# Graph attention kernel: 1,536 of the gathered rows are loaded one by one by SyncE and ScalarE, and the ring of gather buffers has 12 slots in place of 16

## The reference

```python
Q_h = (x @ Wq + bq).reshape(N, H, D)      # K_h, V_h alike
E = (edge_attr @ We + be).reshape(-1, H, D)
score = K_h[src_idx] * Q_h[dst_idx] / jnp.sqrt(D) * E
score = jnp.exp(jnp.clip(score.sum(-1, keepdims=True), -5.0, 5.0))
wV = segment_sum(V_h[src_idx] * score, dst_idx, N)
Z = segment_sum(score, dst_idx, N)
h_out = (wV / (Z + 1e-06)).reshape(N, H * D)
return layernorm(x + h_out)
```

## Time and profile before

| | |
|---|---|
| median of three runs | 1004.61 us |
| profiled execution | 1004.89 us, of it the span of the core 1003.1 us |
| GpSimd busy | 742.9 us (74%), 790 instructions |
| TensorE busy | 754.7 us (75%) |
| VectorE busy | 595.4 us (59%) |
| ScalarE busy | 453.4 us (45%) |
| DMA engines, mean share busy | 50 to 60% through the loop over groups |

### The profile page before, as it was taken

How to read it: one execution, slowest core, us unless ns; L and a number is a source line. 1 busy time by engine, 2 the same in 40 slices (tenths; PEclk the granted TensorE clock), 3 DMA queues, 4 the chain that set the end, 5 groups by cost and what they waited for, 6 DMA issues and landing times.

```text
span 1003.1 us, 13052 instructions
## 1 busy us (share of the span) xinstructions
PE 754.7 (75%) x3387; PEld 418.3 (42%) x3387; DVE 595.4 (59%) x1584; ACT 453.4 (45%) x1096; POOL 742.9 (74%) x790
## 2 busy tenths in 40 slices
PE   5899987877777777777876686777768778777763
PEld 4656643433443334343433343434435334343332
DVE  4459965555555655565556556565565656565664
ACT  3477754444444444444435345334444444444421
POOL 6777777777777777777777777777777777777772
PEclk9999998789789898979788989888887987889885
DMA  8997775555555555555554655555545555555321
GB/s 222 310 238 194 203 190 156 155 152 155 147 150 144 141 155 132 143 137 161 133 148 134 157 141 133 158 133 147 151 129 151 149 150 141 140 141 158 99 80 45
DMA packets 124294, 153.03 MB, mean 153 GB/s; under 512 B 57725, under 2 KB 91967, under 8 KB 124212
## 3 DMA queue, kind: packets, MB, share of 16 engines
q0 software_dynamic: 36944, 75.08, 29.7%
q1 hardware_dynamic: 80448, 73.74, 25.8%
q10 hardware_dynamic: 6822, 3.31, 1.3%
HBM read 142.06 MB, written 9.98 MB: 152 GB/s over the span
## 4 chain that ended last, share of the span: by engine, by line
POOL 64%; issue 21%; PE 5%; DMA 4%; DVE 3%; SPq 1%; ACT 0%; POOLq 0%; DVEq 0%
POOL kv L472 64%; DMA kv<-kv_table,src_idx 2%; DMA q_table<-node_stage 1%; DMA w_all<-biases_in 1%; PE ps_eq L902 1%; PE ps_eq L957 1%; SPq L393 1%; PE ps_qe_seg L902 1%; PE ps_eq L950 1%; DMA q_win<-q_table 1%; PE ps_last L902 0%; DVE node_stage L712 0%; SPq L397 0%; DVE ps_last L737 0%; PE ps_eq_qe L902 0%
## 5 line engine op out<-in xcount | busy, mean ns | idle before, releaser
L472 POOL DMA_INDIRECT kv<-kv_table,src_idx x746 | 706.2, 947 | 227.6 <-issue 225.4
L571 ACT ACTIVATE ps_last<-clipped 128x32 f32<-128x32 f32 x196 | 39.4, 201 | 489.2 <-DVE clipped L744 484.6
L957 PE MATMUL ps_eq<-pick_t,q_win 128*96 128x512 f32 (+1 forms) x262 | 156.3, 682 | 18.8 <-ACT e_t L566 17.5
L950 PE MATMUL ps_eq<-ea,w_all 128*96 128x512 f32 (+1 forms) x262 | 161.4, 703 | 8.2 <-DVE qe_t L720 6.6
L730 DVE TENSOR_TENSOR kq<-kv,ps_qe_seg 128x384 f32<-128x384 f32 x98 | 53.9, 550 | 180.2 <-DMA kv<-kv_table,src_idx 180.0
L730 DVE TENSOR_TENSOR kq<-kv,ps_eq_qe 128x384 f32<-128x384 f32 x98 | 54.1, 552 | 176.4 <-DMA kv<-kv_table,src_idx 176.4
L981 PE MATMUL ps_qe_seg<-node_stage 128*104 128x80 f32 x784 | 104.1, 284 | 52.4 <-DVE acc_t L766 38.0
L981 PE MATMUL ps_last<-node_stage 128*104 128x80 f32 x780 | 99.9, 277 | 56.9 <-DVE acc_t L766 48.2
L557 ACT ACTIVATE distance<-rel_bc,neg_part 80x512 bf16<-80x512 bf16 x196 | 138.4, 706 | 2.0 <-issue 1.0
L560 ACT ACTIVATE pick_t<-distance 80x512 f32<-80x512 bf16 x196 | 123.2, 629 | 6.2
L981 PEld LDWEIGHTS ps_qe_seg<-node_stage 128*104 128x104 f32 x784 | 94.0, 198 | 60.7 <-DVE node_stage L751 45.0
(11 more groups left out here) (85 smaller groups left out, 663.5 us busy)
## 6 DMA issues: line engine op xcount, KB each, us to landing
ea<-ea_t_in SPq DMA_DIRECT2D x196, 192.0 KB
rel_bc<-rel_rows_dram SPq DMA_DIRECT2D x196, 80.0 KB
kv<-kv_table,src_idx POOLq DMA_INDIRECT x746
q_win<-q_table SPq DMA_DIRECT2D x196, 30.0 KB
kv_table<-node_stage SPq DMA_DIRECT2D x5, 960.0 KB, 6.1
x_both<-x_t_in SPq DMA_DIRECT2D x5, 480.0 KB, 12.4
q_table<-node_stage SPq DMA_DIRECT2D x5, 480.0 KB, 7.6
x_both<-x_rows_in ACTq DMA_DIRECT2D x10, 240.0 KB, 3.5
```

Of the source, the lines that this page charges most:

```text
L472: pool.indirect_dma_start(rows[0:n, :], None, table, bass.IndirectOffsetOnAxis(ap=src_idx[0:n, tile:tile + 1], axis=0)).then_inc(semaphore ...
L950: nc.tensor.matmul(ps_eq[2 * group % 3][0:DIM, 0:n], w_e, ea[:, slot, 0:n], start=True, stop=True).then_inc(e_e, 1)
L957: nc.tensor.matmul(ps_eq[(2 * group + 1) % 3][0:DIM, 0:n], q_win[:, slot, :], pick_t[:, group % 3, 0:n], start=True, stop=True).then_inc(e ...
```

## The change

Groups 98 and 190 are no longer gathered by GpSimd. SyncE loads their 1,024 rows, each with a DMA of its own from `kv_table`, 22 in each quad from the first quad on. ScalarE does the same for the 512 rows of group 178, 12 in each quad, three after the exponentials of each group. The node numbers come as two further inputs and are loaded into registers once for each quad. The three groups have buffers and semaphores of their own, and the ring for the 193 groups left to GpSimd has 12 slots. VectorE waits for the four tiles of such a group on four semaphores.

```diff
-KV_RING, EA_RING, REL_RING, QWIN_RING, PICK_RING, MSG_RING = 16, 8, 8, 8, 4, 4
+KV_RING, EA_RING, REL_RING, QWIN_RING, PICK_RING, MSG_RING = 12, 8, 8, 8, 4, 4
+SYNC_GROUPS, SYNC_ROWS = (98, 190), 22
+SCALAR_GROUPS, SCALAR_ROWS = (178,), 12
+ROW_GROUPS = sorted(SYNC_GROUPS + SCALAR_GROUPS)
+POOL_GROUPS = [group for group in range(GROUPS) if group not in ROW_GROUPS]
...
+def rows_in(quad, groups, per_quad):
+    rows = [(group, row) for group in groups for row in range(GROUP)]
+    return rows[quad * per_quad:(quad + 1) * per_quad]
...
+        def load_row(eng, group, row, number):
+            t, p = divmod(row, P)
+            eng.dma_start(kv[p:p + 1, kv_slot(group), t, :], kv_table[bass.ds(number, 1), :]
+                          ).then_inc(e_rows[group][t], 16)
...
 @@ SyncE's loop @@
                 for quad in range(QUADS):
-                    for group, base in enumerate(bases_of(mybir.EngineType.SP, quad), quad * QUAD):
+                    rows = rows_in(quad, SYNC_GROUPS, SYNC_ROWS)
+                    loaded = numbers_of(quad, QUAD + len(rows))
+                    for i in range(QUAD):
...
-                        load_window(group, base)
+                        load_window(group, loaded[i])
+                        for (row_group, row), number in [*zip(rows, loaded[QUAD:])][i::QUAD]:
+                            load_row(sp, row_group, row, number)
...
 @@ GpSimd's loop @@
-                for group in range(EARLY, GROUPS):
-                    slot = group % KV_RING
-                    if group >= KV_RING:
-                        pool.wait_ge(e_msg, group - KV_RING + 1)
+                for i, group in enumerate(POOL_GROUPS[EARLY:], EARLY):
+                    if i >= KV_RING:
+                        pool.wait_ge(e_msg, POOL_GROUPS[i - KV_RING] + 1)
...
 @@ ScalarE's first DMAs, and its loop @@
             act.dma_start(dst_idx[:], dst_cols).then_inc(l_dst, 16)
+            act.dma_start(numbers[:, :, QUAD:], src_sync).then_inc(l_numbers, 16)
+            act.dma_start(act_numbers[:], src_scalar).then_inc(l_act_numbers, 16)
...
                     if group < GROUPS:
                         exponentials(group)
+                    if group % QUAD == 0 and rows_in(group // QUAD, SCALAR_GROUPS, SCALAR_ROWS):
+                        loaded = numbers_of(group // QUAD)
...
+                    for row_group, row in rows_at(group):
+                        load_row(act, row_group, row, loaded.pop(0))
```

More of the change, by code:

```diff
@@ L96, in edges_in, with kv_slot, kv_fetched @@
     return min(P, N_EDGES - tile * P)
+def kv_slot(group):
+    return KV_RING + ROW_GROUPS.index(group) if group in ROW_GROUPS else POOL_GROUPS.index(group) % KV_RING
+def kv_fetched(group):
+    slot, last = kv_slot(group), POOL_GROUPS.index(group)
+    return sum(tiles_of(POOL_GROUPS[i]) for i in range(slot, last + 1, KV_RING))
+def rows_in(quad, groups, per_quad):
+    rows = [(group, row) for group in groups for row in range(GROUP)]
+    return rows[quad * per_quad:(quad + 1) * per_quad]
 def steps_at(group, lag, streamed):
@@ L137, in build @@
     assert SUMS * FINAL_TILES + WINDOW <= 512 and LAG_TRANSPOSE == SUMMED + 2
+    for groups, rows in ((SYNC_GROUPS, SYNC_ROWS), (SCALAR_GROUPS, SCALAR_ROWS)):
+        for i, group in enumerate(groups):
+            assert EARLY <= QUAD * -(-(i + 1) * GROUP // rows) < group < GROUPS - 1
     assert EARLY < KV_RING and tiles_of(EARLY) == GROUP_TILES
@@ L287, in build @@
         e_kv = [sem(f"e_kv{i}") for i in range(KV_RING)]
+        e_rows = {group: [sem(f"e_rows{group}_{t}") for t in range(GROUP_TILES)] for group in ROW_GROUPS}
         e_ea = [sem(f"e_ea{i}") for i in range(EA_RING)]
@@ L540, in _ @@
             act.wait_ge(c_float, 2)
+            act.wait_ge(l_act_numbers, 16)
             path = path_of(act)
@@ L598, in finish_nodes, with numbers_of, rows_at @@
                         normalise(step)
+            def numbers_of(quad):
+                return list(nc.values_load_multi_w_load_instructions(
+                    act_numbers[0:1, quad, 0:len(rows_in(quad, SCALAR_GROUPS, SCALAR_ROWS))],
+                    engines=[mybir.EngineType.Activation], min_val=0, max_val=N_NODES,
+                    skip_runtime_bounds_check_because=IN_TABLES)[1])
+            def rows_at(group):
+                rows = rows_in(group // QUAD, SCALAR_GROUPS, SCALAR_ROWS)
+                first, last = (len(rows) * (group % QUAD + i) // QUAD for i in range(2))
+                return rows[first:last]
             def windowed(streamed):
+                all_tables_stored(act)
                 make_pick_t(0)
@@ L723, in times_keys @@
             def times_keys(group):
-                n, slot = tiles_of(group), group % KV_RING
-                fetched = sum(tiles_of(g) for g in range(slot, group + 1, KV_RING))
-                dve.wait_ge(e_kv[slot], 16 * fetched)
+                n, slot = tiles_of(group), kv_slot(group)
+                if group in ROW_GROUPS:
+                    for t in range(n):
+                        dve.wait_ge(e_rows[group][t], 16 * P)
+                else:
+                    dve.wait_ge(e_kv[slot], 16 * kv_fetched(group))
                 if group < EARLY:
```

33 lines of the change are left out of this document (25 added, 8 removed).

## The result

| | before | after |
|---|---|---|
| median of the runs (12 each), us | 1005.55 | 1001.65 |
| lowest and highest | 1003.4 to 1006.1 | 999.1 to 1003.3 |
| profiled execution / its span | 1004.89 / 1003.1 | 1000.85 / 999.0 |
| start of the first gather from kv_table | 51.85 | 51.84 |
| GpSimd's stalls for a slot | none | 6.68 + 3.26 |

The ratio is 0.996, interval 0.9952 to 0.9968: a gain of 3.9 us, small but clear of the noise, where I had forecast 9.1. The time itself lies in the range (993 to 1004).

The account below looks back on a forecast made before the run. GpSimd's unbroken gathers were taken as the bound: span 1003.1 - 15.0 removed + 5.9 stall at the start = 994.0, with 1.8 beyond the span 995.8, and 0.3 over the median, so forecast 995.5 us; range 993 to 1004.

Parts of the forecast that it names:

- The bound and the removal: GpSimd's gathers run without a pause and set the end; removing 12 at 1.2515 us each saves 15.0 us.
- GpSimd's stalls at the start: GpSimd stands still once, before its 13th gather, for 5.9 us, with bounds of 4.2 and 7.5.
- The ring alone: With 12 slots, GpSimd's 13th gather waits until group 0 is weighed: 4.2 us.
- The rows ahead of the first windows: 17 row DMAs at 0.51 us on SyncE delay group 3's query window to 67.3, lengthening the stall to 5.7 us.
- The register load: SyncE's load of 26 numbers in each quad, taken as 0.6 us, between 0.3 and 1.9.
- later groups don't wait: After the start GpSimd asks for one slot in 5.0 us, and slots come free in 2.78 or 4.4.
- SyncE through the loop: SyncE's work for a quad sums to 17.7 us (bounds 14.6 and 21.7), hidden behind GpSimd's 20.0.
- B: Rival: SyncE becomes the bound in the loop, slower once a quad takes 19.2 to 19.4 us; 1011 at 19.5; chance 0.14.
- D: Rival: rows and loads on ScalarE push `e_t` past VectorE's need in part of the groups, 998 to 1003; chance 0.06.
- C: Rival: all single rows meet on one DMA engine, slower if a row costs over 0.27 us; 1038 at 0.30; chance 0.04.
- ScalarE's rows: Three rows a group on ScalarE cost 1.3 to 1.9 us, at most 4.3 of 5.0 busy, so nothing in time.
- The ends: The 18.0 us behind the last gather stay as they are, though groups 178 and 190 cost no gather time.

Follow-up runs that it names:

- e8: e7 with a ring of 14 slots and the number tables in partition 96 of other tiles, rows of 28 numbers: 990.12 us, ratio 0.9856.
- h3: Kernel before with only group 178 loaded by single rows, three a group on ScalarE, and a ring of 15: 999.98 us, ratio 0.9952.
- h2: e8 with a second group (134) on ScalarE, six rows a group: 985.20 us, ratio 0.9811.
- e5: Kernel before with a ring of 12 slots and nothing else changed: 1011.07 us, ratio 1.0066.
- e7: e6 with SyncE's rows starting only in the third quad, 24 a quad instead of 22: 997.47 us, ratio 0.993.
- e6: Changed kernel with each quad's row of SyncE's numbers padded from 26 to 32 (128 bytes): 998.06 us, ratio 0.9928.
- k2: e8 with the table of SyncE's numbers moved by 4 bytes: 1578 us, ratio 1.178, in a session whose times decide nothing.
- k1: e8 with the table of SyncE's numbers moved by 8 bytes: 1592 us, ratio 1.189, in a session whose times decide nothing.

## Why the prediction was wrong

**The bound and the removal: right.** GpSimd's gathers set the end, and 12 x 1.2515 = 15.0 us are really gone; e8 shows them nearly whole, h3 and h2 four at a time.

**The failed step: GpSimd's stalls at the start, 5.9 us in the sum, 9.9 measured.** Its parts:
- The ring alone, priced at 4.2 us from the earlier trace rows, measured 6.65 (e5) and 5.0 (e7). I took one execution's start for the start, and it was the shortest of the nine in the table: 19.2 us from the first gather to the end of group 0's weighing, where the others have 19.8 to 24.9. The first gather varies by 3 us over the profiles, and TensorE's clock in the first steps between its two levels. With a slack that covers it the variation has no price, and the change removed that slack.
- The rows ahead of the first windows: from the window of group 0 to that of group 3 it is 66.85 - 57.83 = 9.02 us, before 1.54, so the 17 rows took 7.5, 0.44 each, where I had priced 8.7. The first window went out 1.04 later than before, where I had priced 0.3, because of the longer first load (1.87 us). So that of group 3 went out at 66.85, forecast 67.3. Its product on VectorE still began later than forecast, 70.79 against 70.1, and not for the sake of that window: TensorE worked without a pause from 62.47, where it had the first window, until it had picked group 3's query rows, with a granted clock of 0.56 in 62 to 65 and 0.87 in 65 to 68. So the first stall is 6.68, not 5.9. e5 has 6.65 without any rows: what the rows themselves cost is less than starts differ by.
- **The register load, priced at 0.6 us with 1.9 as its upper bound: 2.1 and 5.5 measured.** The first load is 1.87, which is my upper bound; the second, at 5.5, is far beyond it. I had no row for it, chose near the load of one number (0.478), and asked only what the count does, never what the address does. This one load is the second stall, 3.26 us, which I did not have at all ("later groups don't wait"). e6 takes the long loads out and the second stall with them. Some 0.9 us of the 3.26 are TensorE's clock: it had fallen to 1.2 GHz in the pause that the load made (0.50 in 78 to 81), and the pair of matmuls that picks group 4's query rows took 2.02 us, that of group 3 1.02.
- The Trainium skill ("Runtime: NRT & Kernel Launch", Instruction fetch mechanics) has about 200 ns for each register, of registers loaded from HBM; here they come from SBUF. I set that aside since four numbers took 298 ns. Here 26 numbers take 0.08 us each on an aligned row (2.10) and 0.21 each on the others (5.54), so its figure fits the second kind alone.

**A small term that wasn't there.** The loop's gathers are 0.0015 us longer each, 1.1 us. e8, with as many rows, doesn't have it. Over the nine profiles the mean step from gather to gather without the stalls lies between 1.2506 (e8) and 1.2530 (the changed kernel), and 1.2520 in e5 without any rows, so part of it may be no more than the difference between executions; its cause is open.

**SyncE through the loop: right in sum, wrong in its terms.** 17.7 us a quad forecast, 18.87 measured: rows 9.1 instead of 11.2, loads 3.9 in the mean instead of 0.6. That is 0.3 short of the 19.2 from which B was to decide. It did not decide (no stall behind 82 us, and e6's shorter quad gave no more than its stall), but the VectorE waits show how thin the cover had become: 12.2 us of waiting for gathers left of 356.4. Had the row been 0.51 as priced, the quad would have come to 21. B's price itself stays untested.

**Two signs named for rivals came without them.** VectorE waited 315.6 us for `e_t`, which I had named for D, and TensorE 143.1 us for `ea`, which I had named for B. Both come from SyncE's lateness, and neither cost anything while GpSimd had free slots. The waits of the engine that sets the end would have been the sign to name.

**C and D.** One DMA engine for all rows (C) would lengthen gathers' landing and bring slots late in the loop; with six plus six rows a group in h2, GpSimd never stalls. The trace has the price: each row is one packet of 768 bytes and one of 4 (SyncE's queue has 82,496 - 80,448 = 2 x 1,024 packets more than before), and the 512 of ScalarE's queue took 0.047 us of a DMA engine each in the mean, where C needed over 0.27. Which engine ran them the profile doesn't tell. ScalarE's rows cost nothing (h3), as forecast, at 0.40 us from row to row in the median.

**The ends.** The tail behind the last gather, taken as it was, is 18.8 against 18.9. Groups 178 and 190, which cost no gather time near the end, didn't lengthen it.

## What to carry to other kernels

Where one engine runs without a pause and sets the end, a stall of it anywhere is lost for good, at the start as much as in the loop: write the whole time as first start + count x interval + stalls + tail, and ask of a change that moves work off it whether the ring still covers its start in a bad execution, not in the one profiled. A ring's spare slots are what hides such variation; before they are spent, look for other room, such as unused partitions of a tile.

Where a cost hangs on data layout as well as on count, the nearest row of another layout is no bound.

A chain of waits that passes through an engine with almost the pace of the bound proves nothing about which of the two decides; pauses of the suspected bound do, and a kernel that changes only the other engine.

## What the runs showed of the hardware

- A load of registers from SBUF on SyncE takes 0.30 us for 4 numbers (before), 1.9 for 28 (e8) and 2.1 for 26 (e6), 0.07 to 0.08 each, if its first address is a multiple of 16 bytes. At 4 (k2) or 8 bytes (k1) past one, 28 numbers take 5.92, and at 8 past 26 take 5.5 (the changed kernel). Why 26 aligned numbers take longer than 28 is open. On ScalarE 12 aligned numbers take 0.96; on VectorE 4 take 0.34 aligned (e8) and 0.96 at 8 past (k1).
- A single row of 768 bytes with its address in a register costs the issuing engine's queue 0.41 us on SyncE and 0.40 on ScalarE in the median (the changed kernel), 0.23 of it the DMA's issue itself. SyncE issued 1024 and ScalarE up to 1024 of them (h2) beside 730 gathers with no sign of one DMA engine filling up.
- TensorE's granted clock was at 1.2 GHz for some 3 us of the first steps in some executions (e5: 0.50 in 62 to 65, after pauses of 1.55 and 0.97 us) and at 2.4 GHz in others with the same instructions ahead of it (before: 1.00, after pauses of 1.59 and 0.20). The same pair of matmuls took 2.02 us at the one and 1.10 at the other.
